# B of steps 2 to 14 turned by transposing DMAs instead of TensorE, with its low part made on GpSimd

## The reference

```python
proj = einsum('bsd,ed->bse', x, in_proj_w)             # gate, hs, B, C, dt
hBC  = silu(causal_conv4(hBC))                          # hs: 128 heads x 64; B, C: 8 groups x 128
Bc, Cc = B, C by chunks of 128 tokens
Y_diag = einsum('bzlhn,bzshn,bhzls,bzshp->bzlhp', Cc, Bc, L, xch)
states = einsum('bzlhn,bhzl,bzlhp->bzhpn', Bc, decay_states, xch)
Y_off  = einsum('bzlhn,bzhpn,bhzl->bzlhp', Cc, prev, exp(A_cum))
y = (Y_diag + Y_off + hs * D) * silu(gate)              # then a norm in groups, and out_proj
```

## Time and profile before

| | |
|---|---|
| median of 3 runs | 1625.42 us (1623.97 to 1625.75) |
| the profiled execution | 1625.32 us, of which its span is 1624.0 us |
| PE busy | 1601.9 us, 99% of the span |
| PE load, DVE, ACT, POOL busy | 80%, 84%, 77%, 82% |
| granted TensorE clock | 0.996 of full, 1.00 in every stretch read here |
| DMA: share of 16 engines | 50.3% |

### The profile page before, as it was taken

The page is one execution under the profiler, slowest core; times in us unless marked ns, Lnnn a source line. Parts: engine busy times, 40 slices in busy tenths (PEclk is TensorE's granted clock), DMA queues, the critical chain, the costliest instruction groups (busy, mean ns, idle before and its releaser), DMA issues.

```text
span 1624.0 us, 31886 instructions
## 1 busy us (share of the span) xinstructions
PE 1601.9 (99%) x10792; PEld 1305.4 (80%) x10792; DVE 1371.1 (84%) x1665; ACT 1253.0 (77%) x2643; POOL 1337.9 (82%) x1240
## 2 busy tenths in 40 slices
PE   8998999999999999999999999999999999999999
PEld 7776888888888888888888888888888888888777
DVE  5978789887988879898798978988798887989788
ACT  5177787887878788787877878788787878778774
POOL 3157689996899879898799968999688987999796
PEclk9999999999999999999999999999999999999999
DMA  4162355554555554444645446545564465645453
GB/s 134 54 209 97 116 170 179 164 150 134 158 156 140 163 156 146 124 143 139 192 148 138 125 139 186 150 134 150 150 165 119 130 167 161 177 121 133 133 163 105
DMA packets 216387, 236.12 MB, mean 145 GB/s; under 512 B 154273, under 2 KB 155809, under 8 KB 212001
## 3 DMA queue, kind: packets, MB, share of 16 engines
q1 hardware_dynamic: 216224, 234.07, 50.3%
HBM read 147.51 MB, written 55.05 MB: 125 GB/s over the span
## 4 chain that ended last, share of the span: by engine, by line
PE 90%; DVE 4%; POOL 2%; issue 2%; ACT 1%; DMA 0%; SPq 0%; POOLq 0%; DVEq 0%; ACTq 0%
PE P L268 8%; PE P L269 8%; PE P L270 8%; PE P L514 8%; PE P L364 7%; PE P L347 7%; PE P L365 7%; PE P L371 7%; PE P L354 7%; PE P L348 7%; PE P L379 4%; PE P L500 2%; PE P L497 1%; PE P L498 1%; PE P L488 1%
## 5 line engine op out<-in xcount | busy, mean ns | idle before, releaser
L624 ACT ACTIVATE P<-AB,SC 128x128 f32<-128x128 f32 x1008 | 303.9, 360 | 20.6 <-DVE EM L1018 20.5
L268 PE MATMUL P<-xh,AH 128*128 128x512 f32 x656 | 263.4, 401 | 1.7 <-DVE hsX L887 1.5
L887 DVE SCALAR_TENSOR_TENSOR hsX<-P,cwt,hsX 128x1023 f32<-128x1023 f32 x189 | 241.7, 1279 | 26.8 <-ACT hsX L555 22.3
L269 PE MATMUL P<-xl,AH 128*128 128x512 f32 x656 | 256.9, 392 | 0.0
L270 PE MATMUL P<-xh,AL 128*128 128x512 f32 x656 | 256.8, 391 | 0.0
L347 PE MATMUL P<-GH,xh 128*128 128x512 f32 x512 | 211.7, 413 | 0.0
L364 PE MATMUL P<-OH,gTh 128*128 128x512 f32 x508 | 199.4, 392 | 2.5 <-issue 2.4
L348 PE MATMUL P<-GH,xl 128*128 128x512 f32 x512 | 200.8, 392 | 0.0
L365 PE MATMUL P<-OH,gTl 128*128 128x512 f32 x508 | 197.8, 389 | 0.0
L1245 POOL TENSOR_TENSOR AL<-AR,AH 128x512 fp32r<-128x512 f32 x82 | 110.3, 1345 | 80.6 <-ACT AH L542 80.6
L1274 POOL TENSOR_TENSOR DL<-dxh,DH 128x512 fp32r<-128x512 f32 x112 | 173.3, 1547 | 0.0
(11 more groups left out here) (229 smaller groups left out, 4174.8 us busy)
## 6 DMA issues: line engine op xcount, KB each, us to landing
AB<-acr_d SPq DMA_DIRECT2D x128, 512.0 KB, 4.7
half_d<-hsX SPq DMA_DIRECT2D x60, 512.0 KB, 3.7
AR<-in_wa SPq DMA_DIRECT2D x80, 256.0 KB, 2.7
TS<-in_wg SPq DMA_DIRECT2D x16, 1024.0 KB, 5.2
TS<-in_wo SPq DMA_DIRECT2D x16, 1024.0 KB, 6.7
part_d<-pl SPq DMA_DIRECT2D x64, 256.0 KB, 3.2
pl<-part_d SPq DMA_DIRECT2D x64, 256.0 KB, 3.6
SC<-sct_d SPq DMA_DIRECT2D x16, 128.0 KB, 5.2
```

The source lines that it names most:

```text
L268: te.matmul(o, ah_, bh_, start=(first and i == 0), stop=False)
L269: te.matmul(o, ah_, bl_, start=False, stop=False)
L624: r = se.activation(decays(m)[:, h, :], AB[m % 2][:, h, :], ACT.Relu, bias=SC[s % 2][:, c, 3, h:h + 1], scale=-1.0)
L887: ve.scalar_tensor_tensor(out=o[:, d:T], in0=raw[:, 0:T - d], scalar=cwt[:, n, 3 - d:4 - d], in1=o[:, d:T], op0=ALU.mult, op1=ALU.add).the ...
```

## The change

Of the seven even steps 2 to 14:

- B's tile is split in 16-bit halves like the H tiles (one more ACT copy, POOL copy and store by SP a step, into a new DRAM tensor `bhalf_d`), and each of its 8 chunks is brought back by a transposing DMA into BT[m % 2], issued right behind the one into HT. It waits for BL of m - 2, and its arrival is counted in the same semaphore `ht_in`, so that xch, dxh and dhs now wait for both.
- PE makes no transpose of B (56 fewer); ACT makes BH from BT, in SBUF, and waits for `ht_in` instead of `s_bg`.
- BL is no longer made by DVE, from PSUM, ahead of Gt; POOL makes it from BT and BH, behind dhs at the end of `pool_front`.
- Turned tiles are numbered anew (H and B together), and the waits that count them follow.

```diff
@@ pe_front
-                te.transpose(o[:, 0:128], Bx[:, tok(c)], ident[:, :])
+                if s == 0:
+                    te.transpose(o[:, 0:128], Bx[:, tok(c)], ident[:, :])
                 te.matmul(o[:, 128:256], Bx[:, tok(c)], Cx[:, tok(c)], start=True, stop=True).then_inc(s_bg, 1)
@@ act_front
-                se.wait_ge(s_bg, ngc(m))
+                if s:
+                    se.wait_ge(ht_in[m % 2], nht(m))
+                    se.wait_ge(s_x, 1 + tile_no["C", s])
+                else:
+                    se.wait_ge(s_bg, ngc(m))
...
-                se.activation(BH[:, c, :], bank("BG", m)[:, 0:128], ACT.Copy).then_inc(s_bh, 1)
+                se.activation(BH[:, c, :], BT[m % 2][:, :] if s else bank("BG", m)[:, 0:128], ACT.Copy).then_inc(s_bh, 1)
@@ dve_blocks
-                ve.wait_ge(s_bh, ngc(m))
-                if s and c != 7:
-                    ve.wait_ge(s_stp, n7(m - 8))
-                ve.tensor_tensor(BL[:, c, :], o[:, 0:128], as_f(BH[:, c, :]), ALU.subtract).then_inc(s_bl, 1)
+                if s == 0:
+                    ve.wait_ge(s_bh, ngc(m))
+                    ve.tensor_tensor(BL[:, c, :], o[:, 0:128], as_f(BH[:, c, :]), ALU.subtract).then_inc(s_bl, 1)
+                ve.wait_ge(s_bg, ngc(m))
@@ dve_scaled, pool_scaled, pool_front
-                ve.wait_ge(ht_in[m % 2], 16 * (m // 2 - 3))
+                ve.wait_ge(ht_in[m % 2], nht(m))
@@ pool_front, behind dhs
+            if s and s % 2 == 0:
+                pe_.wait_ge(s_bh, ngc(m))
+                if c != 7:
+                    pe_.wait_ge(s_stp, n7(m - 8))
+                pe_.tensor_tensor(BL[:, c, :], BT[m % 2][:, :], as_f(BH[:, c, :]), ALU.subtract).then_inc(s_bl, 1)
@@ sp_halves
-            sp.dma_start(half_d[(n // 4 + 1) % 2, n % 4], low_high).then_inc(half_st[n % 4], 16)
+            t = ctiles[i]
+            sp.dma_start(half_d[t[1] % 2, t[2]] if t[0] == "H" else bhalf_d, low_high).then_inc(half_st[n % 4], 16)
@@ sp_turned
             sp.dma_start_transpose(HT[m % 2].bitcast(u16), rows[:, tok(c)]).then_inc(ht_in[m % 2], 16)
+            if s % 2 == 0:
+                sp.wait_ge(s_bl, ngc(m) - 2)
+                rows = bhalf_d.rearrange("p b t -> (p b) t")
+                sp.dma_start_transpose(BT[m % 2][:, :].bitcast(u16), rows[:, tok(c)]).then_inc(ht_in[m % 2], 16)
```

More of the change, by code:

```diff
@@ L20, in mamba_moe_block_kernel @@
     half_d = nc.dram_tensor("half_d", [2, 4, 128, 2, T], u16, kind="Internal").ap()
+    bhalf_d = nc.dram_tensor("bhalf_d", [128, 2, T], u16, kind="Internal").ap()
     eal_d = nc.dram_tensor("eal_d", [NS, 8, NC], f32, kind="Internal").ap()
@@ L107, in nsa, with turns_of, nht @@
         return 6 * (m // 8) + m % 8
+    turned = [i for i, t in enumerate(ctiles) if t[0] == "H" and t[1] or t[0] == "B" and t[1]]
+    turn_no = {i: n for n, i in enumerate(turned)}
+    def turns_of(s):
+        return sum(1 for i in turned if ctiles[i][1] <= s)
+    def nht(m):
+        return 16 * sum(2 if n // 8 % 2 == 0 else 1 for n in range(m, 7, -2))
     ctx = ExitStack()
@@ L134, in mamba_moe_block_kernel @@
         BL = sb("BL", [128, NC, 128], f32r)
+        BT = [sb(f"BT{i}", [128, 128]) for i in range(2)]
         SC = [sb(f"SC{i}", [128, NC, 4, 8]) for i in range(2)]
@@ L286, in turned_no @@
         def turned_no(i):
-            t = ctiles[i]
-            return 4 * (t[1] - 1) + t[2] if t[0] == "H" and t[1] else None
+            return turn_no.get(i)
         tanh5 = (EM[1][:, 0:512], th[:, 512:1024])
@@ L547, in act_tap @@
             se.wait_ge(s_half, 2)
-            if t[0] == "H" and t[1] and turned_no(i) > 1:
-                se.wait_ge(s_hi, turned_no(i) - 1)
-                se.wait_ge(s_lo, turned_no(i) - 1)
+            if t[0] == "H" and t[1]:
+                p_ = tile_no.get(("H", t[1] - (t[2] < 2), (t[2] + 2) % 4))
+                if p_ in turn_no:
+                    se.wait_ge(s_hi, turn_no[p_] + 1)
+                    se.wait_ge(s_lo, turn_no[p_] + 1)
             elif t[0] != "H" and t[1] > 0:
@@ L554, in act_tap @@
                 se.wait_ge(s_cl, 4 * t[1])
+                if t[1] > 2 and t[0] == "B":
+                    se.wait_ge(s_lo, turn_no[tile_no["B", t[1] - 2]] + 1)
             se.activation(tile_out(i), pair("A", i), ACT.Identity, bias=cbt[:, n:n + 1], scale=cwt[:, n, 3:4]).then_inc(s_tap, 1)
@@ L1263, in pool_scaled @@
             if s:
-                pe_.wait_ge(ht_in[m % 2], 16 * (m // 2 - 3))
+                pe_.wait_ge(ht_in[m % 2], nht(m))
             else:
@@ L1417, in sp_turned @@
             if c == 0:
+                n_ = turns_of(s)
                 for j in range(4):
-                    sp.wait_ge(half_st[j], 16 * s)
+                    sp.wait_ge(half_st[j], 16 * ((n_ + 3 - j) // 4))
             sp.wait_ge(s_dhs, m - 1)
```

## The result

The changed kernel takes 1639.12 us (median of 4 runs, 1638.20 to 1640.66), before 1624.70 (4 runs, 1623.61 to 1625.75). The ratio is 1.0088, 95% interval 1.0076 to 1.0100: 14.4 us slower. The forecast was 6.2 us slower, within a range that reached to 1642. The way was right, the size was less than half.

The account below looks back on a forecast made before the run. PE was taken as the bound, with POOL's unbroken chain beside it in even steps; 1625.3 + 5.0 (POOL's late BL, PE's gain of 7.2 already in it) + 1.2 (late transposing DMA) = 1631.5 us, range 1619 to 1642.

Parts of the forecast that it names:

- PE is the bound, a transpose costs 0.11 us: On PE, busy 1601.9 of 1624.0 us: each of 56 removed transposes saves 0.11 us, 6.2 us in all.
- The place at O(31), 0.14 us a step: PE's O(31) waits for Gt to free its bank; Gt coming 0.20 earlier regains 0.14 us, 1.0 us over seven steps.
- POOL is an unbroken chain, and BL makes St of chunk 2 late: First five chunks of even steps: added BLs delay POOL, and PE waits 1.06 us at St(34).
- each BL at 0.47: On POOL: BL takes 0.47 us, the median of 64 like operations CL, whose worst case is 1.44.
- no collision: On POOL: no BL is assumed held by DVE's two-input operations; half of a possible 7 us kept for the range.
- the rival that gains: POOL's chain shortens if its collisions with DVE disappear, so PE only gains: 1618.1 us; chance 0.15.
- the 11.4 that it names: PE's stalls at St of chunks 2 and 3: 7 x 1.63 = 11.4 us.
- Chunk 3, 0.57 us a step: PE's St(35) waits 0.57 us for POOL's BL, ready at 543.95 against 543.38 wanted, in each even step.
- BT lands late at chunk 5, 1.2 us in three steps: BT's DMA arrives 2.5 us later, delaying Gt(37); PE's O(34) waits 0.8 us in step 4, 1.2 in all.
- The halves of B, the DMAs: POOL and ACT copies and store of B's halves fall in an odd step's fifth chunk, under cover: no cost.
- BL is held by DVE: On POOL: one of four BLs a step meets a two-input DVE operation, + 6.8 us, 1638.3 us; chance 0.08.

Follow-up runs that it names:

- the order alone: The kernel before, with DVE making BL and Gt ahead of dxh and B still turned by PE: 1621.33 us, ratio 0.9964.
- the long wait: The kernel before, with PE's St of chunk 2 of steps 2 to 14 also waiting for POOL's low-half copy behind OL: 1647.70 us, ratio 1.0147.

## Why the prediction was right in its way and wrong in its size

- **PE is the bound, a transpose costs 0.11 us.** Right: every chunk without a wait gains 0.10. The gain in all is 6.7 us (6.0 outside chunk 2, and 0.7 in it); the forecast had 7.2.
- **The place at O(31), 0.14 us a step.** It gave 0.28, as the order alone did in the kernel before: the gap between matmuls went from 0.37 to 0.23, and the first matmul behind the gap was longer too.
- **POOL is an unbroken chain, and BL makes St of chunk 2 late.** Right, and shown: with BL behind DL the wait goes, with everything else in place. This is the step whose size failed. I took "each BL at 0.47", "no collision"; two of the three took 0.87 from start to next start, held by dxh, and PE came 0.2 earlier. The wait cost 2.3 us (2.2 of it idle) instead of 1.06, seven times 1.24, some 9 us. The 0.2 of PE are the larger gain at O(31) and a slip: four transposes stand ahead of St(34), not three (step 4's are at 493.78, 504.71, 515.92 and 527.53). With the fourth the wait of the prediction is 1.17 and its stalls are 7 x 1.74 = 12.2, less the gain of 7.2, which is its 5.0; with the 11.4 that it names they would be 4.2. The rows gave a warning: OL behind dhs of chunk 2 took 1.74 instead of 1.30, and I used it for the rival that gains. (AL behind dhs of chunk 3 took 1.75 as well, but BL(35) there took 0.48; so such a row tells that holds happen, not which operation will meet one.) A median over 64 places was the wrong number for a place where a neighbour was already being held.
- **The clock.** Not in the prediction in any form. Five stretches at half clock, 1.6 us each (3.8 - 2.2), 8 us. That is the second step that failed, a cost put at nothing: what PE loses behind a wait. That the wait is the cause is shown by the long wait in the kernel before. That length matters is suggested, not shown to be all: at chunk 2 no wait of 1.6 us or less brought it, and of the 14 with 1.9 to 2.4 us idle nine did.
- **Chunk 3, 0.57 us a step.** It did not come: PE was later from chunk 2 on, BL(35) was ready at 544.84, and St(35) started at 547.06, 0.23 behind the matmul before it. (The 0.3 that chunk 3 loses in steps 4 and 8 are at the output projection behind St.) With a shorter wait at chunk 2 it comes: where BL stands between the decay and dhs, chunk 3 loses 0.4 in each step, and the 0.1 of the transpose.
- **BT lands late at chunk 5, 1.2 us in three steps.** It did not come in the change, because PE and ACT were late already. Once PE is on time it comes: 0.7 us in steps 4, 8 and 12 with BL behind DL. The term was right and covered by the larger one.
- **The halves of B, the DMAs.** Nothing, as forecast: 0.02 us in the steps.
- **The rivals and the range.** "BL is held by DVE" (0.08) had the mechanism, and its 1638.3 lies next to the 1639.1 measured, by luck: it had one long hold a step where two short ones came, the waits of chunks 3 and 5, which did not come, and no clock. Nor is it to the credit of the range that it reached to 1642; that end was made of collisions and late transposes, and 8 us of what came are the clock.

The sum as it came, in the steps: 7 x 2.32 (waits) + 5 x 1.57 (clock) - 6.7 = 17.4 us; the medians differ by 14.4, of which I can say only that the stretch ahead of step 1 varies by some us from run to run and in the profiles lay 1.7 us ahead in the changed kernel.

Open: why steps 6 and 14 escape the low clock with the same wait, and steps 4, 8 and 12 in the kernel with the long one.

## What to carry to other kernels

Work moved to an engine is paid at the place where it stands in that engine's chain: read there how near its results come to the bound's needs, and take the durations of the neighbours at that place, not a median. When the bound is TensorE, a wait of some 2 us can cost more than its length, since the granted clock may halve behind it; so cut one long wait before several short ones. Removing PE work ahead of a wait can make a kernel slower, as it did here. And an operation that no longer depends on a slow one should be moved ahead of it at once: here that order alone gave 2.3 us in the steps, and with the change 2.7.

## What the runs showed of the hardware

- TensorE's granted clock fell from 2.4 to 1.2 GHz for 3.4 us behind 5 of 7 waits with 2.0 us idle, behind 4 of 7 with 1.9 to 2.4 us (a wait of 2.43 us among those without, one of 1.93 among those with it), and behind none with 1.6 us (8 waits), 1.2 (7) or 1.0 and less (14), in otherwise full stretches. It fell between 1.4 us after PE had gone on, as in the windows above, and 0.4 us before, as in the long wait of step 2, where the first matmul is already slow.
- DVE's subtraction of 128x128 took 278 ns with one input in PSUM and 1135 ns (median of 56, up to 1383) with both in SBUF beside a busy POOL. On POOL it took 472 (median, up to 933), and the long ones stood beside DVE's dxh, from two tiles in SBUF.
- A transposing DMA of 256 rows by 128 took 1.23 us to issue on SP's queue, of 1024 rows 1.16 at best (the transposes of hs, median 1.44, up to 3.99 in the kernel before): at these two sizes the issue time hardly goes with size. The smaller one landed 2.8 us after its issue (median).
